# A 128-token output product of the last stage cut into four column tiles of 32 tokens

## The chip, the core and the metric

The kernel runs on one core of a Trainium2 chip. The core has a matrix engine (PE, with a separate record PEld for the loading of its stationary operand), three elementwise engines (DVE, ACT, POOL), and a DMA queue issued by SyncE (SP). The metric is the device time of one execution in microseconds (us); lower is better.

## The reference

The input is 8192 tokens of 512 channels, all float32. What is computed, cut to its core:

```
h = layernorm(x) * (1 + ca) + sa
y = state_space_scan(h)                 # one 16 x 16 recurrence for each channel
y = gelu(layernorm(y)*ln_w + ln_b)
x = x + ga * (h + y @ W_out.T + b_out)  # the first output product is y @ W_out.T
h = layernorm(x) * (1 + cb) + sb
x = x + gb * ffn(h)                     # 512 -> 64 channels, 16 relus for each, -> 512
```

ca, sa, ga, cb, sb, gb come from a small product of silu(c) with a 512 x 3072 matrix.

## The kernel before

The first stages (until about 488 us) turn the scan into matrix products: powers of the 16 x 16 matrices, taps, states at chunk borders, and a banded product for each channel. They leave y for all tokens in SBUF.

The last stage runs over 32 units u of 256 tokens, two tiles t of 128 tokens each. It is a software pipeline written out by hand: each engine has its own list in program order, and semaphores tie them. ACT normalises y (L512), PE transposes it (`t_y`, L1019, line 1019), ACT applies gelu into `zT` (L520, channels on partitions, tokens in columns). PE then forms the first output product, `out1` (L1029): for each tile of 128 tokens, four matmuls over the four groups q of 128 channels, stationary operand `zT` (128 channels x 128 tokens), moving operand `WoT` (128 channels x 512 outputs), accumulated in one PSUM bank, 2 + t, with the tokens on the partitions. DVE adds the residual (L798). The second half normalises again (L529), transposes (`t_x`, L1052), multiplies by a 512 x 64 matrix (`s_prod`, L1062), evaluates 16 relus (ACT L547, DVE L828), and multiplies by the 64 x 512 matrix (`out2`, L1071). Biases are added by bfloat16 matmuls of 32 rows (`bias_pair`, L1037 and L1041; L1075).

PE's list for unit u is: out1 of tile 0 (q = 0 to 3); transposes `t_x` of unit u - 2; out2 and its bias of unit u - 6; out1 of tile 1, q = 0, 1; transposes `t_y` of unit u + 1, first half; the bias pair; out1 of tile 1, q = 2, 3; `t_y`, second half; and after every odd unit from 3 on, `s_prod` of two units. Parts whose unit does not exist are left out at both ends.

A matmul addresses a part of PE's 128 x 128 array. The trace writes that part as rows*columns: 128*128 is the whole array, 128*32 a column tile 32 wide, whose output lies on 32 PSUM partitions; 128*64 is half the columns; 64*128 and 32*128 are row tiles, for products over 64 or 32 channels. Every float32 matmul shows as two records in the trace, called passes here, each with its own weight load; a bfloat16 one shows as one.

Of the kernel before, what the change touches and what calls it, by code (L numbers as in the profile page):

```python
# [12 lines left out]
P = 128  # L13
# [18 lines left out]
QB = D // P  # L32
# [12 lines left out]
BR = 32  # L45
# [13 lines left out]
def adaln_ssm_kernel(nc, x_in, A_in, Bm_in, Cm_in, Dm_in, lnw_in, lnb_in, Wo_in, bo_in,  # L59
# [12 lines left out]
    with ctx:  # L72
# [15 lines left out]
        def pair_of(i):  # L88
            return XY[:, :, i, :, :].rearrange("p b c a -> p b (c a)")

        def channel(d):
            return XY[:, :, d // 2, :, d % 2]
# [51 lines left out]
        zT = A0[:, 0:2048].rearrange("p (r q t) -> p r q t", r=2, q=QB)  # L144
# [9 lines left out]
        WoT = C0[:, 2048:4096].rearrange("p (q d) -> p q d", q=QB)  # L154
# [27 lines left out]
        PS = ctx.enter_context(nc.psum_tensor("PS", [P, 8, 512], f32))  # L182

        def pv_ps(r):
            return PS[:, 2 * r:2 * r + 2, :].rearrange("p b (s w) -> p (b s) w", w=128)

        def w_ps(r):
            return PS[:, 4 + r, :].rearrange("p (g w) -> p g w", w=64)
# [673 lines left out]
        def _(pe):  # L862
# [16 lines left out]
            for half in range(HALVES):  # L879
# [4 lines left out]
                for n in range(STEPS):  # L884
# [10 lines left out]
                    for j in range(8):  # L895
                        g = 8 * o + j
                        for e in QD:
                            pe.matmul(pv_ps(r)[e:e + BW, j, 0:w + NS], BDTs[e:e + BW, b, j, :], PV[e:e + BW, g, PW - w:PW + NS],  # L898
                                      start=True, stop=True)
                        for e in QD:  # L900
                            mm = pe.matmul(w_ps(r)[e:e + BW, j, 0:w], BDs[e:e + BW, b, j, :], WP[e:e + BW, g, L + 1 - w:L + 1],  # L901
                                           start=True, stop=True)
# [4 lines left out]
                for b in range(2):  # L907
                    for m in range(4):
                        for e in range(4):
                            g = (4 * b + e) * 4 + m  # L910
                            mm = pe.matmul(PS[32 * e:32 * e + 32, 4, b * P:(b + 1) * P], CM[:, g, :], PV[:, g, 0:L],
                                           start=(m == 0), stop=(m == 3))
# [3 lines left out]
                for g in range(HG):  # L916
                    for e in QD:
                        mm = pe.matmul(PS[e:e + BW, 5, g:g + 1], BDs[e:e + BW, (base + STEPS + g // 8) % BDR, g % 8, :],
                                       WP[e:e + BW, g, L:L + 1], start=True, stop=True)
# [14 lines left out]
                for q in range(8):  # L934
# [6 lines left out]
                    for i in range(4):  # L941
                        for e in range(4):
                            d = (half * HG + 4 * q + i) * GC + 2 * e
                            mm = pe.matmul(PS[32 * e:32 * e + 32, q % 4, i * P:(i + 1) * P],
                                           Uring[:, q % 2, i * P + 32 * e:i * P + 32 * e + 32], pair_of(d // 2),
                                           start=True, stop=True)
                    mm.then_inc(S["u_mm"], 1)
                    if q == 4:
                        pe.wait_ge(S["ksa_r"], 2 * (half + 1))
                        for b in range(2):  # L950
                            mm = pe.transpose(PS[:, 4, HD + b * P:HD + (b + 1) * P], ktsa[:, b, :], ident[:, :])
# [6 lines left out]
                for i in range(SSTEPS):  # L958
# [6 lines left out]
                    for j in range(8):  # L965
                        g = 8 * o + j
                        for e in QD:
                            mm = pe.matmul(pv_ps(n % 2)[e:e + BW, j, 0:NS + NC], BDTs[e:e + BW, n % BDR, j, :],  # L968
                                           PV[e:e + BW, g, H0:PW + NS], start=True, stop=True)
# [4 lines left out]
                for g in range(HG):  # L974
                    n = half * HG + g
                    if half == HALVES - 1 and 6 <= g < 6 + QB:
                        q = g - 6
# [3 lines left out]
                        for o in range(QB):  # L981
                            mm = pe.transpose(PS[:, 6 + q % 2, o * P:(o + 1) * P], WoN[:, o, q * P:(q + 1) * P], ident[:, :])
                        mm.then_inc(S["wo_tr"], 1)
                    if half == HALVES - 1 and g == 18:

                        pe.wait_ge(S["ld_w"], 16 * 15)
                        for r in range(2):
                            for q in range(QB):
                                mm = pe.matmul(PS[64 * r:64 * r + 64, 5, 0:1], WinS[:, q, :], cbsb[:, 4 + q:5 + q], start=(q == 0), stop=(q == QB - 1))
# [9 lines left out]
                    for h in range(GC):  # L999
                        for a in range(0, P, 64):  # L1000
                            mm = pe.matmul(PS[a:a + 64, g % 4, h * NC:(h + 1) * NC], Tring[:, n % 3, h, a:a + 64], channel(n * GC + h),  # L1001
                                           start=False, stop=(h == GC - 1), skip_group_check=True)
# [19 lines left out]
            def out1(u, t, qs):  # L1022
                n = TPU * u + t
                if t == 1 and qs[0] == 0 and u >= 1:
                    pe.wait_ge(S["x2_r"], n - TPU + 1)
                for q in qs:
                    if t == 0 and q % 2 == 0:
                        pe.wait_ge(S["gelu_r"], QB * u + q + 2)
                    mm = pe.matmul(PS[:, 2 + t, :], zT[:, u % 2, q, t * P:(t + 1) * P], WoT[:, q, :], start=(q == 0 and t == 1),  # L1029
                                   stop=(q == QB - 1))  # L1030
                if qs[-1] == QB - 1:
                    mm.then_inc(S["o1_mm"], 1)

# [46 lines left out]
            for u in range(NU + LAG):  # L1080
                w = u - 1
                if u < NU:
                    out1(u, 0, (0, 1, 2, 3))
                if 1 <= w <= NU:
                    t_x(w - 1, 0)
                    t_x(w - 1, 1)
                if u >= LAG:
                    out2(u - LAG)
                if u < NU:
                    out1(u, 1, (0, 1))  # L1090
                if u + 1 < NU:
                    t_y(u + 1, 0)
                if u < NU:
                    bias_pair(u)
                    out1(u, 1, (2, 3))
                if u + 1 < NU:
                    t_y(u + 1, 1)
                if w % 2 == 0 and 2 <= w <= NU:
                    s_prod(w - 2)
                    s_prod(w - 1)  # L1100
# [33 lines left out]
```

## Time and profile before

| | |
|---|---|
| three runs | 897.92, 901.37, 901.39 us; median 901.37 |
| the profiled execution's own time | 900.21 us |
| its span, first to last instruction | 898.5 us (1.7 us lie around it) |
| PE busy / weight loads busy | 823.3 us (92%) / 553.7 us (62%) |
| DVE, ACT, POOL busy | 570.9, 415.2, 487.9 us |
| mean granted clock of TensorE | 0.909 |
| L1029, passes | 512 |

The span is from the first to the last instruction. A start in the trace is a time measured; the end of a matmul is modelled and reaches into the next one, so that the durations of adjoining PE rows overlap. To know what a group of matmuls occupies, subtract its start from the start of the next row.

### The profile page before, as it was taken

How to read it: one execution, taken by the hardware profiler on the slowest of the kernel's cores; microseconds unless marked ns; L12 is line 12 of the kernel's file. 1: busy time of each engine (PE TensorE's matmuls, PEld its weight loads, DVE VectorE, ACT ScalarE, POOL GpSimd, SP SyncE). 2: the span in 40 equal slices, each digit the busy share in tenths (PEclk: the TensorE clock that was granted, in tenths of full speed). 3: DMA queues.
4: the chain of work that ended last, by engine and by line, in shares of the span. 5: the costliest groups of instructions: out<-in, count | busy, mean ns of one | idle time of the engine just before them, and what ended most of it. 6: DMA issues, size and time to landing. Idle time of an engine off the chain costs nothing.

```text
span 898.5 us, 24744 instructions
## 1 busy us (share of the span) xinstructions
PE 823.3 (92%) x10139; PEld 553.7 (62%) x10139; DVE 570.9 (64%) x1264; ACT 415.2 (46%) x887; POOL 487.9 (54%) x643
## 2 busy tenths in 40 slices
PE   1999978999979999888995999999999999999983
PEld 1967876866669999686663455555555455555540
DVE  5768658833331224883479347877787777777765
ACT  2645632100001113210000569788777788777763
POOL 3634441744433233174443989777777777777500
PEclk9999779999975558999998899999999999999975
DMA  8954302059820000206985220222222222221112
GB/s 249 392 165 148 94 6 85 3 150 249 243 56 3 2 2 4 61 3 191 272 232 184 82 94 2 94 94 94 92 81 87 94 87 79 95 93 48 47 71 94
DMA packets 109808, 94.88 MB, mean 106 GB/s; under 512 B 14976, under 2 KB 81152, under 8 KB 109696
## 3 DMA queue, kind: packets, MB, share of 16 engines
q1 hardware_dynamic: 109696, 93.31, 32.8%
q8 instruction: 80, 1.31, 0.6%
q14 instruction: 32, 0.26, 0.1%
HBM read 75.99 MB, written 17.30 MB: 104 GB/s over the span
## 4 chain that ended last, share of the span: by engine, by line
PE 77%; DVE 11%; DMA 3%; issue 3%; POOL 2%; ACT 2%; SPq 1%; DVEq 0%; POOLq 0%; ACTq 0%
PE PS L1029 26%; PE PS L898 9%; PE PS L901 7%; PE PS L1001 5%; PE PS L996 4%; PE PS L968 4%; PE PS L1062 4%; PE PS L1071 4%; PE PS L1019 3%; PE PS L876 3%; PE PS L1052 3%; DMA arenaC<-kernel_taps 2%; DVE arenaA L750 2%; DVE arenaA L756 1%; DVE arenaC L640 1%
## 5 line engine op out<-in xcount | busy, mean ns | idle before, releaser
L1029 PE MATMUL PS<-arenaC,arenaA 128*128 128x512 f32 x512 | 244.0, 610 | 0.0
L358 POOL TENSOR_TENSOR arenaC<-arenaA,par 128x512 f32<-128x512 f32 x104 | 107.7, 1040 | 145.9 <-ACT arenaA L482 70.5
L898 PE MATMUL PS<-arenaA,arenaC 64*64 64x17 f32 (+6 forms) x1792 | 160.3, 261 | 23.8 <-DVE arenaC L640 23.8
L898 PEld LDWEIGHTS PS<-arenaA,arenaC 64*64 64x64 f32 x1792 | 136.4, 192 | 29.2 <-issue 24.4
L901 PE MATMUL PS<-arenaA,arenaC 64*64 64x1 f32 (+6 forms) x1792 | 152.2, 239 | 0.0
L1029 PEld LDWEIGHTS PS<-arenaC,arenaA 128*128 128x128 f32 x512 | 90.1, 190 | 94.2 <-issue 89.7
L901 PEld LDWEIGHTS PS<-arenaA,arenaC 64*64 64x64 f32 x1792 | 137.4, 192 | 0.0
L828 DVE SCALAR_TENSOR_TENSOR PS<-arenaA,ffc,PS 128x256 f32<-128x256 f32 x224 | 109.2, 487 | 41.5 <-ACT arenaA L547 22.7
L640 DVE STREAM_TRANSPOSE arenaC<-arenaC 128x512 f32<-128x512 f32 x104 | 73.5, 707 | 93.1 <-POOL arenaC L358 92.0
L547 ACT ACTIVATE arenaA<-PS,ffc 128x256 f32<-128x256 f32 x256 | 124.9, 582 | 8.8 <-PE PS L1062 7.8
L408 POOL TENSOR_TENSOR arenaC<-arenaA,mask 128x504 f32<-128x504 f32 x64 | 65.9, 1031 | 77.2 <-PE PS L996 74.8
L652 DVE TENSOR_TENSOR XY<-PS,arenaA 128x256 f32<-128x256 f32 x128 | 48.4, 420 | 77.3 <-PE PS L1001 76.9
L1001 PEld LDWEIGHTS PS<-XY,arenaC 128*64 128x64 f32 x2048 | 65.9, 136 | 51.0 <-issue 34.9
L520 ACT ACTIVATE arenaA<-PS,lnwb 128x256 f32<-128x256 f32 x128 | 65.9, 575 | 52.4 <-PE PS L1019 52.3
L512 ACT ACTIVATE arenaC<-XY,sy 128x512 f32<-128x512 f32 x64 | 49.2, 821 | 83.0 <-POOL sy L344 83.0
L424 POOL TENSOR_TENSOR ROWS<-ROWS 128x512 f32<-128x512 f32 x64 | 81.5, 1273 | 5.3
L1001 PE MATMUL PS<-XY,arenaC 128*64 128x64 f32 x2048 | 74.8, 224 | 2.2 <-DMA arenaC<-kernel_taps 2.2
L996 PE MATMUL PS<-arenaC,arenaA 128*128 128x512 f32 x128 | 71.6, 641 | 1.6 <-DVE arenaA L1109 1.6
L480 ACT ACTIVATE arenaA<-PS 128x128 f32<-128x128 f32 x56 | 15.5, 278 | 122.3 <-PE PS L901 122.3
L968 PE MATMUL PS<-arenaA,arenaC 64*64 64x80 f32 x1536 | 60.4, 231 | 11.3 <-DVE arenaA L1109 5.9
L968 PEld LDWEIGHTS PS<-arenaA,arenaC 64*64 64x64 f32 x1536 | 56.5, 133 | 15.7 <-issue 11.0
L1019 PEld LDWEIGHTS PS<-ident,arenaC 128*128 128x128 f32 x256 | 32.5, 143 | 43.3 <-issue 43.3
(154 smaller groups left out, 1206.0 us busy)
## 6 DMA issues: line engine op xcount, KB each, us to landing
arenaC<-kernel_taps SPq DMA_DIRECT2D x64, 512.0 KB, 4.3
arenaC<-in_L_attn_x SPq DMA_DIRECT2D x32, 256.0 KB, 4.4
XY<-in_L_attn_x SPq DMA_DIRECT2D x32, 256.0 KB, 4.4
arenaC<-in_L_attn_x SPq DMA_DIRECT2D x15, 512.0 KB, 3.5
out<-arenaC SPq DMA_DIRECT2D x15, 512.0 KB, 2.7
XY<-in_L_wmod SPq DMA_DIRECT2D x6, 1024.0 KB, 8.1
XY<-in_L_attn_x SPq DMA_DIRECT2D x11, 512.0 KB, 3.6
out<-XY SPq DMA_DIRECT2D x11, 512.0 KB, 2.8
```

What stands on the lines that cost most here:

```text
L358: gp.tensor_tensor(BDs[:, step % BDR, :, :].rearrange("p g (a m) -> p g a m", m=NS), src, msk, ALU.mult).then_inc(S["bdp_r"], 1)
L408: gp.tensor_tensor(BDH[:, g % 2, :, 1:NC], PV[:, g, H0:H0 + NC - 1].unsqueeze(1).to_broadcast([P, GC, NC - 1]), mask8[:, :].unsqueeze(2).t ...
L424: chain(gp.tensor_tensor(tmp, tmp, Grow, ALU.mult))
L547: act.activation(rr[:, h % RELU_RING, :], PS[:, 5, 0:FP * P], ACT.Relu, scale=W1c[:, h:h + 1], bias=b1c[:, h:h + 1]).then_inc(S["relu_r"], 1)
L640: dve.transpose(BDTs[:, step % BDR, :, :], BDs[:, step % BDR, :, :]).then_inc(S["bdt_r"], 1)
L828: ins = dve.scalar_tensor_tensor(out=dst, in0=rr[:, h % RELU_RING, :], scalar=W2c[:, h:h + 1], in1=g, op0=ALU.mult, op1=ALU.add)
L898: pe.matmul(pv_ps(r)[e:e + BW, j, 0:w + NS], BDTs[e:e + BW, b, j, :], PV[e:e + BW, g, PW - w:PW + NS], start=True, stop=True)
L901: mm = pe.matmul(w_ps(r)[e:e + BW, j, 0:w], BDs[e:e + BW, b, j, :], WP[e:e + BW, g, L + 1 - w:L + 1], start=True, stop=True)
L968: mm = pe.matmul(pv_ps(n % 2)[e:e + BW, j, 0:NS + NC], BDTs[e:e + BW, n % BDR, j, :], PV[e:e + BW, g, H0:PW + NS], start=True, stop=True)
L996: pe.matmul(PS[:, g % 4, :], WP[:, g, 0:L], BDH[:, g % 2, :, :], start=True, stop=False, skip_group_check=True).then_inc(S["o_mm"], 1)
L1001: mm = pe.matmul(PS[a:a + 64, g % 4, h * NC:(h + 1) * NC], Tring[:, n % 3, h, a:a + 64], channel(n * GC + h), start=False, stop=(h == GC - ...
L1029: mm = pe.matmul(PS[:, 2 + t, :], zT[:, u % 2, q, t * P:(t + 1) * P], WoT[:, q, :], start=(q == 0 and t == 1), stop=(q == QB - 1))
```

## The change

Each matmul of `out1`, with its 128 tokens, becomes four matmuls in a loop over a = 0, 32, 64, 96. Each takes 32 columns of `zT` as its stationary operand and the same 512 outputs of `WoT` as its moving operand, and writes PSUM partitions a to a + 31 of the same bank. The four go to four column tiles of the array. Bias, semaphores, the flags for the start and stop of an accumulation, and the other engines' lists are as they were. The loop covers both tiles t of every unit: 256 matmuls become 1024.

```
                 for q in qs:
                     if t == 0 and q % 2 == 0:
                         pe.wait_ge(S["gelu_r"], QB * u + q + 2)
-                    mm = pe.matmul(PS[:, 2 + t, :], zT[:, u % 2, q, t * P:(t + 1) * P], WoT[:, q, :], start=(q == 0 and t == 1),
-                                   stop=(q == QB - 1))
+                    for a in range(0, P, BR):
+                        mm = pe.matmul(PS[a:a + BR, 2 + t, :], zT[:, u % 2, q, t * P + a:t * P + a + BR], WoT[:, q, :],
+                                       start=(q == 0 and t == 1), stop=(q == QB - 1))
                 if qs[-1] == QB - 1:
                     mm.then_inc(S["o1_mm"], 1)
```

PE's list before, in an even unit of the steady state, from the first matmul of `out1` of tile 0 to the transposes after the second half of tile 1 (the numbers after the tile names are the output's partitions x its columns; brackets name semaphores waited for):

```order
L1029 MATMUL PS<-arenaC,arenaA 128x512 [waits gelu_r]
L1029 MATMUL PS<-arenaC,arenaA 128x512
L1029 MATMUL PS<-arenaC,arenaA 128x512 [waits gelu_r]
L1029 MATMUL PS<-arenaC,arenaA 128x512
L1052 MATMUL PS<-ident,arenaA 128x128 [waits gelu_r,xh2_r]
...
L1075 MATMUL PS<-bcs,ones_bf 128x512 x2
L1029 MATMUL PS<-arenaC,arenaA 128x512 [waits x2_r]
L1029 MATMUL PS<-arenaC,arenaA 128x512
L1019 MATMUL PS<-ident,arenaC 128x128 [waits xT_r,yh_r]
```

The same places of PE's list in the changed kernel, where the lines from `out1` on have a number one higher:

```order
L1030 MATMUL PS<-arenaC,arenaA 32x512 [waits gelu_r]
L1030 MATMUL PS<-arenaC,arenaA 32x512 x7
L1030 MATMUL PS<-arenaC,arenaA 32x512 [waits gelu_r]
L1030 MATMUL PS<-arenaC,arenaA 32x512 x7
L1053 MATMUL PS<-ident,arenaA 128x128 [waits gelu_r,xh2_r]
...
L1076 MATMUL PS<-bcs,ones_bf 128x512 x2
L1030 MATMUL PS<-arenaC,arenaA 32x512 [waits x2_r]
L1030 MATMUL PS<-arenaC,arenaA 32x512 x7
L1019 MATMUL PS<-ident,arenaC 128x128 [waits xT_r,yh_r]
```

Nothing changes its place and no wait is added. Each block of `out1` has four times the instructions, of another shape than the transposes on either side of it.

## Rows read from the trace of the kernel before

**Rows 1.** The page: busy share, and the clock, in 40 slices of the span.
```profile
PE   1999978999979999888995999999999999999983
...
PEclk9999779999975558999998899999999999999975
```

**Rows 2.** Busy time of every engine in stretches of the last stage; start:end length, engines, clock.
```profile
core 0: us, PE busy (x) PEld busy (x) DVE busy (x) ACT busy (x) POOL busy (x), PEclk, DMA share, GB/s
...
500.00:600.00 100.00, 100.00 (x437) 51.86 (x436) 68.00 (x147) 74.70 (x138) 86.34 (x116) 1.00 0.17 56
...
800.00:858.00 58.00, 58.00 (x262) 29.13 (x260) 42.20 (x88) 45.24 (x87) 36.75 (x50) 1.00 0.16 57
```

**Rows 3.** Waits from 480 to 870 us: waiter <- waited for: us, times, longest.
```profile
ACT arenaA L520 <- PE PS L1019: 52.3, 46, 5.1
...
DVE arenaC L798 <- PE PS L1029: 25.9, 14, 8.4
```

**Rows 4.** PE in order of time, two units of the steady state: start, us, what, count.
```profile
600.17 0.60 PE L1019 MATMUL PS<-ident,arenaC 128*128 128x128 f32 x4
600.70 1.97 PE L1062 MATMUL PS<-arenaA,WinS 128*64 128x128 f32 x32
602.60 3.70 PE L1029 MATMUL PS<-arenaC,arenaA 128*128 128x512 f32 x8
606.13 1.04 PE L1052 MATMUL PS<-ident,arenaA 128*128 128x128 f32 x8
607.10 1.13 PE L1071 MATMUL PS<-ROWS 64*128 64x512 f32 x4
...
611.15 1.98 PE L1029 MATMUL PS<-arenaC,arenaA 128*128 128x512 f32 x4
612.97 0.60 PE L1019 MATMUL PS<-ident,arenaC 128*128 128x128 f32 x4
613.41 3.60 PE L1029 MATMUL PS<-arenaC,arenaA 128*128 128x512 f32 x8
616.84 1.04 PE L1052 MATMUL PS<-ident,arenaA 128*128 128x128 f32 x8
```

**Rows 5.** PE in order of time, the products in four column tiles (L944).
```profile
142.45 1.08 PE L944 MATMUL PS<-XY,arenaC 128*32 128x128 f32 x32
143.46 0.44 PE L951 MATMUL PS<-ident,arenaC 128*128 128x128 f32 x2
...
370.55 0.66 PE L927 MATMUL PS<-ident,arenaA 128*128 128x128 f32 x4
371.13 1.95 PE L944 MATMUL PS<-XY,arenaC 128*32 128x128 f32 x64
373.02 0.70 PE L955 MATMUL PS<-arenaC,WinS 128*128 128x256 f32 x2
```

**Rows 6.** Weight loads of the same stretch.
```profile
371.13 1.69 PEld L944 LDWEIGHTS PS<-XY,arenaC 128*32 128x32 f32 x64 [0.17 <-issue]
```

**Rows 7.** PE in order of time, the products in two column tiles (L1001).
```profile
476.44 1.16 PE L1001 MATMUL PS<-XY,arenaC 128*64 128x64 f32 x32
477.54 1.12 PE L996 MATMUL PS<-arenaC,arenaA 128*128 128x512 f32 x2
```

**Rows 8.** PE in order of time, the early units, without out2.
```profile
518.29 1.04 PE L1052 MATMUL PS<-ident,arenaA 128*128 128x128 f32 x8
519.16 1.88 PE L1029 MATMUL PS<-arenaC,arenaA 128*128 128x512 f32 x4
520.88 0.60 PE L1019 MATMUL PS<-ident,arenaC 128*128 128x128 f32 x4
```

**Rows 9.** PE in order of time, the end of the last unit.
```profile
856.55 1.98 PE L1029 MATMUL PS<-arenaC,arenaA 128*128 128x512 f32 x4
858.47 1.97 PE L1062 MATMUL PS<-arenaA,WinS 128*64 128x128 f32 x32
860.37 1.09 PE L1052 MATMUL PS<-ident,arenaA 128*128 128x128 f32 x8
861.39 1.13 PE L1071 MATMUL PS<-ROWS 64*128 64x512 f32 x4
```

**Rows 10.** The chain that ended last: start, us, what.
```profile
858.54 1.92 PE PS L1062 x32
860.48 1.21 ACT arenaA L547 x3
```

## The prediction

> **What bounds the kernel now.** I read the slices of the page first. From the stage's start at about 494 us to about 860 us PE stands at nine tenths or more in every slice, and the clock is at its upper level, 2.4 GHz, except in the slice where the stage starts and in those of the drain [rows 1]. Next the busy times by stretch: from 500 to 858 us PE is busy for every microsecond at a granted clock of 1.00, DVE at 68 to 73%, ACT at 75 to 78%, POOL at 63 to 86% [rows 2]. A PE that is busy by modelled ends is not yet a PE that bounds, so I asked who waits for whom: ACT's gelu waits for PE's transposes for 52.3 us, and DVE's residual for this very product for 25.9 us [rows 3]. Then PE in order of time, by starts. A block of eight passes of L1029 takes 616.84 - 613.41 = 3.43 us, 0.43 us a pass; four passes of a transpose take 613.41 - 612.97 = 0.44 us, 0.11 us a pass [rows 4]. 512 and 128 columns at two cycles of 2.4 GHz each are 0.427 and 0.107 us, so PE streams without a bubble. The other engines follow it, and what PE's list gains or loses here goes to the span unchanged. At the end nothing takes it back: the chain leaves PE at the last L1062, and the relus of ACT start from its end [rows 10].
>
> **What an even spread over column tiles costs.** The work streamed is unchanged: 256 matmuls of 128 tokens become 1024 of 32, and 512 passes become 2048, in 512 groups of four that should run side by side. The nearest rows are L944, the same form with 128 columns in place of 512, four tiles of 128*32. 32 passes take 143.46 - 142.45 = 1.01 us and 64 take 373.02 - 371.13 = 1.89 us [rows 5]. The 32 passes more are eight groups, 0.88 / 8 = 0.11 us a group, just what one pass over the whole array takes for 128 columns [rows 4]. Four column tiles share neither the array nor the stream. So a group of four with 512 columns should take the 0.43 us of one pass now, and the stream costs nothing. Extrapolating the length by four is my choice; the trace has no column tile with 512 columns. Its lower bound is the same 0.43, for no tiled row streams a column in less than two cycles (the pairs of L1001, 64 columns, take about 0.056 us: 1.10 us less 0.2 for the change of shape, over 16 pairs [rows 7]). Its upper bound I take from the start to start distance that four tiles would add if it weren't overlapped, 0.02 us a group, 10 us in all; L944 shows none of it in 16 groups.
>
> **What the changes of shape cost.** Here the rows speak plainly.
> Leaving a shape: four transposes before another L1029 take 0.44 us, four before L1062, which uses the array as 128*64, take 600.70 - 600.17 = 0.53 [rows 4]. A change costs 0.09 us, though both shapes have all 128 rows.
> Entering one: the first weight load of the new shape isn't hidden. L1029 after L1062 takes 606.13 - 602.60 = 3.53 us for eight passes, against 3.43 after transposes: 0.10 us [rows 4]. Transposes after L1062 take 861.39 - 860.37 = 1.02 us [rows 9], after L1029 607.10 - 606.13 = 0.97 [rows 4], both before the same L1071: 0.05 us.
> A block in four column tiles: twice 1.01 less 1.89 leaves 0.13 us a block, for its entry and its exit together [rows 5]. Of it 0.09 is the change at its end; 0.04 is the short load of 32 columns and the four starts apart.
>
> The Trainium skill says the same in TensorEngine Tiling (Array Packing), Key Properties, and it speaks against this change: going from one tile to another of the same mode is free, a change of the mode drains TensorE. It gives no price. By that rule alone, at the 0.09 us of the row, the new changes of shape listed below (21 at an entry, 92 at an exit, of which the tiled block's 0.13 holds its own) would cost 10.2 us, near my sum.
>
> **The sum.** PE's list has 94 blocks of `out1`: 2 of 12 passes (units 0 and 1), 30 of 8 (tile 0), 62 of 4 (tile 1). Four groups:
> 71 blocks come today after another shape (57 after the biases, 14 after L1062) and before transposes of their own shape. They pay 0.10 at the entry today and 0.13 afterwards: 71 x 0.03 = 2.1 us.
> 21 come after transposes of the same shape: the 12 of unit 1, 16 of the blocks of 8, and 4 of the early units, where no out2 stands between (1.72 us for four passes, nothing beside the stream [rows 8]). The transposes ahead of them now pay 0.09 for leaving and the block 0.13, where nothing was paid: 21 x 0.22 = 4.6 us.
> 2 in the last unit stand between two changes already: 858.47 - 856.55 = 1.92 us for four passes, 0.20 over the stream [rows 9]; 0.13 in its place gives back 0.1 us.
> 92 are followed by transposes, which pay 0.05 for their own first load: 4.6 us.
> Together 2.1 + 4.6 - 0.1 + 4.6 = 11.2 us. Starts are rounded to 0.01 us, so the sum could be about 1 us off either way. The first block runs at the lower clock, which doubles one entry and is nothing. All of it lies on PE's list between 497 and 860 us, beside nothing. Nobody else is queued anew: ACT's and DVE's lists are the same, and both have slack. The sum is against the profiled execution's 900.21 us: 911.4. The runs' median, 901.37, lies 1.2 us above that execution, so the median of the changed kernel should come out near 912.5, which I forecast.
> Bounds: below, if the transposes' load is hidden after all (4.6 less) and the exit costs what it does from 128*64, 907 from the same base; above, with 0.02 us a group lost to the stagger, 922.
>
> **The rivals.**
> Weight loads stand in line. The four tiles use the same 128 rows, and if a load can't pass running matmuls that use these rows, each of the 418 groups inside a block would wait for it: L944's 0.04 us a block, less the starts apart, is about 0.03 us a load, 12 us more, 924. For it: nothing in a row. Against it: L944's 64 loads lie within 1.69 us, under 64 passes that take no longer than their stream [rows 5, 6]; a pair of L1001 with two loads of 64 columns takes 0.056 us, so loads run side by side as well [rows 7]. Chance 5%.
> The Trainium skill has the rule behind this rival, in TensorE: Matmul & The Clock Gate, Part 3: a weight load overlaps running matmuls only where the row group differs. Here no row group differs; by the rule the time would be 924, and L944 disagrees with it.
>
> The streams don't fit four abreast. L944 reads 128 columns at a time; with 512 the four streams might serialise into two pairs. Every group would take 0.86 us: 512 x 0.43 = 220 us more, 1130. L944's stream is without a gap over 16 groups, and I see no reason for a longer one to differ. Chance 2%.
>
> It gets faster. The one saving in the rows is the entry: the load of a 32-column tile exposes 0.03 to 0.04 us where the whole width exposes 0.10, at 73 blocks, about 5 us. If going into and out of a column tile drained nothing, and the transposes' load hid under the last streams, only that saving would be left: 901.4 - 5 = 896. It decides if an exit and the load behind it cost under about 0.02 us together. Against it: 128*128 to 128*64 is such a change of columns alone, and costs 0.09 [rows 4]; L944 holds 0.13 a block [rows 5]. Chance 2%.
>
> PE's extra time falls into waits: then 901. PE waits for nobody here by its starts, so only the tail could hide it, and that starts from PE [rows 10]. Chance 2%.
>
> A partial cover, some loads hidden beside the drain, gives 905 to 908. Chance 8%. My forecast, with 908 to 917 around it, has the remaining 81%.
>
> **Range and chances.** 8 in 10 with both near neighbours: 907.5 to 920. A measurement of this kernel tells 0.5% from nothing, 4.5 us. Slower: forecast, partial cover but for its lower edge, weight loads in line and serial streams, 95%. Same: 3%, hidden time and that edge. Faster: 2%.
>
> **What would show it.** In the profile after: 2048 passes of 128*32 for the product; eight groups of four in a block of tile 0 from start to start in about 3.43 + 0.13 = 3.56 us, before and after s_prod alike, where it is 3.53 or 3.43 now; the transposes ahead of it 0.53 in every unit; the transposes after it 0.05 longer than now; two units together about 0.7 us longer; PE still 100% busy between 500 and 865 us at a clock of 1.00; the time from the end of the last block of the product to the end of the span as long as now, 898.5 - 858.5 = 40 us. If a block of tile 0 takes 3.8 us, it is the loads; if 7, the streams. I am wrong if a block of eight groups takes under 3.4 us, or if PE shows waits for ACT or DVE in the steady state.

## The result and the profile after

Four runs of the changed kernel took 909.03 to 914.06 us, median 912.06; four of the kernel before, on the same chip, 897.92 to 901.39, median 900.45. The ratio is 1.0131, 95% interval 1.0093 to 1.0168: slower by 1.3%, 11.6 us between the medians. The profiled execution took 912.76 us, its span 911.0 (before 900.21 and 898.5). The forecast was a median of 912.5.

The busy times by stretch, of the changed kernel (columns as in [rows 2]):

```profile
500.00:600.00 100.00, 100.00 (x874) 38.56 (x868) 63.17 (x137) 70.93 (x131) 83.30 (x114) 1.00 0.16 57
...
800.00:858.00 58.00, 58.00 (x510) 23.89 (x513) 41.81 (x90) 45.73 (x87) 42.24 (x58) 1.00 0.16 56
```

They answer to [rows 2]: PE is still never idle, at a granted clock of 1.00. In the first stretch ACT and DVE have a smaller share than before, since they do the same work behind a slower PE. PEld falls from 51.86 to 38.56 us there, and that is no gain: loads under running passes cost nothing before either.

The waits in the changed kernel from 480 to 880 us (total, times, longest), and then the product's group before and after (busy us, mean ns | idle before):

```profile
ACT arenaA L520 <- PE PS L1019: 61.4, 48, 4.8
DVE arenaC L798 <- PE PS L1030: 28.0, 14, 8.1
```

```profile
L1029 PE MATMUL PS<-arenaC,arenaA 128*128 128x512 f32 x512 | 244.0, 610 | 0.0
L1030 PE MATMUL PS<-arenaC,arenaA 128*32 128x512 f32 x2048 | 240.2, 599 | 0.0
```

ACT waits 9 us longer for PE than in [rows 3]. The product's own busy time went *down*, 244.0 to 240.2 us, while the kernel got slower: a busy time of modelled ends says nothing here. What does is the starts, PE in order of time, in the changed kernel:

```profile
605.83 0.66 PE L1019 MATMUL PS<-ident,arenaC 128*128 128x128 f32 x4
606.42 1.97 PE L1063 MATMUL PS<-arenaA,WinS 128*64 128x128 f32 x32
608.31 3.64 PE L1030 MATMUL PS<-arenaC,arenaA 128*32 128x512 f32 x32
611.88 1.09 PE L1053 MATMUL PS<-ident,arenaA 128*128 128x128 f32 x8
612.91 1.13 PE L1072 MATMUL PS<-ROWS 64*128 64x512 f32 x4
...
614.29 1.92 PE L1030 MATMUL PS<-arenaC,arenaA 128*32 128x512 f32 x16
616.14 0.66 PE L1019 MATMUL PS<-ident,arenaC 128*128 128x128 f32 x4
...
618.91 0.66 PE L1019 MATMUL PS<-ident,arenaC 128*128 128x128 f32 x4
619.50 3.64 PE L1030 MATMUL PS<-arenaC,arenaA 128*32 128x512 f32 x32
623.07 0.66 PE L1053 MATMUL PS<-ident,arenaA 128*128 128x128 f32 x4
```

Subtract each start from the next, and compare with [rows 4]. Eight groups of four take 611.88 - 608.31 = 3.57 us behind s_prod (3.53 before) and 623.07 - 619.50 = 3.57 behind transposes (3.43 before). Four groups take 1.85. So 4 more groups take 3.57 - 1.85 = 1.72 us, 0.43 each: the four tiles run abreast for 512 columns too, and each block pays 0.14 once. Eight transposes behind the product take 1.03 (0.97 before). Four of them take 0.59 ahead of another shape; between two blocks of the product they took 0.44.

The weight loads show the entry directly. First the kernel before, then the changed one, in both the first loads of `t_x` (L1052, L1053) behind the product:

```profile
605.71 0.14 PEld L1052 LDWEIGHTS PS<-ident,arenaA 128*128 128x128 f32 x1 [0.24 <-issue]
606.13 0.80 PEld L1052 LDWEIGHTS PS<-ident,arenaA 128*128 128x128 f32 x7 [0.29 <-issue]
```

```profile
611.88 0.86 PEld L1053 LDWEIGHTS PS<-ident,arenaA 128*128 128x128 f32 x8 [0.84 <-issue]
```

Before, the first of the eight loads starts at 605.71, under the product's last pass and 0.42 us ahead of the first transpose at 606.13. Behind the column tiles no load starts early: all eight stand at or behind the first transpose at 611.88.

For the comparisons below I use one stretch of steady state, 28 units: from the second half of unit 4's transposes to the end of the last block of the product. Its ends, first in the kernel before, then in the changed one:

```profile
532.69 0.49 PE L1019 MATMUL PS<-ident,arenaC 128*128 128x128 f32 x3
...
858.47 0.33 PE L1062 MATMUL PS<-arenaA,WinS 128*64 128x128 f32 x2
```

```profile
535.83 0.44 PE L1019 MATMUL PS<-ident,arenaC 128*128 128x128 f32 x2
...
872.03 0.44 PE L1063 MATMUL PS<-arenaA,WinS 128*64 128x128 f32 x4
```

325.78 us before, 336.20 after: 10.42 us in 14 pairs of units, 0.74 a pair. Of the span's 12.5 us, 1.5 more lie in the first units of the stage, 1.6 in the stages ahead, which the change doesn't touch, and the tail is 1.0 shorter (39.0 for 40.0). Those last two are of the size by which executions of the same code differ there. In the six profiled executions of before, after, e1, e2a, e2b and e3 the code ahead of the stage is the same, and the stage's first transpose starts between 494.55 and 499.14 us; in all of these but e3 the tail's code is the same too, and it took 38.3 to 40.0 us. So the steady stretch is the better ruler: where PE has no gap, nearly all blocks of the same kind in the same surroundings agree to 0.01 us.

### The profile page after: what moved, and what is told of

Its sections match the earlier page's. It is cut to its first block, busy times and chain, and to the rows that moved or that the text cites. A ratio compares the mean times of both kernels' runs of the same rounds, so it can differ in the third digit from the quotient of the medians.

```text
span 911.0 us, 27816 instructions
## 1 busy us (share of the span) xinstructions
PE 837.8 (92%) x11675; PEld 517.4 (57%) x11675; DVE 571.0 (63%) x1264; ACT 416.7 (46%) x887; POOL 489.0 (54%) x643
## 4 chain that ended last, share of the span: by engine, by line
PE 80%; DVE 10%; issue 3%; DMA 2%; POOL 2%; ACT 2%; SPq 1%; DVEq 0%; POOLq 0%; ACTq 0%
PE PS L1030 26%; PE PS L898 10%; PE PS L901 7%; PE PS L1001 5%; PE PS L996 5%; PE PS L968 4%; PE PS L1019 4%; PE PS L1072 3%; PE PS L1063 3%; PE PS L1053 3%; PE PS L876 3%; DVE arenaA L750 2%; DMA arenaC<-kernel_taps 1%; DVE arenaA L756 1%; DVE arenaC L640 1%
## 5 line engine op out<-in xcount | busy, mean ns | idle before, releaser
L1030 PE MATMUL PS<-arenaC,arenaA 128*32 128x512 f32 x2048 | 240.2, 599 | 0.0
L898 PE MATMUL PS<-arenaA,arenaC 64*64 64x17 f32 (+6 forms) x1792 | 163.7, 265 | 21.1 <-DVE arenaC L640 21.1
L901 PE MATMUL PS<-arenaA,arenaC 64*64 64x1 f32 (+6 forms) x1792 | 155.2, 242 | 0.0
L898 PEld LDWEIGHTS PS<-arenaA,arenaC 64*64 64x64 f32 x1792 | 138.8, 195 | 26.6 <-issue 23.1
L901 PEld LDWEIGHTS PS<-arenaA,arenaC 64*64 64x64 f32 x1792 | 140.0, 196 | 0.0
L1030 PEld LDWEIGHTS PS<-arenaC,arenaA 128*32 128x32 f32 x2048 | 57.0, 109 | 117.3 <-issue 111.5
L1001 PEld LDWEIGHTS PS<-XY,arenaC 128*64 128x64 f32 x2048 | 66.0, 136 | 50.7 <-issue 35.7
L1001 PE MATMUL PS<-XY,arenaC 128*64 128x64 f32 x2048 | 74.9, 224 | 2.0 <-DMA arenaC<-kernel_taps 1.8
L996 PE MATMUL PS<-arenaC,arenaA 128*128 128x512 f32 x128 | 71.6, 641 | 1.6 <-DVE arenaA L1110 1.6
L480 ACT ACTIVATE arenaA<-PS 128x128 f32<-128x128 f32 x56 | 15.5, 277 | 124.7 <-PE PS L901 124.7
L968 PEld LDWEIGHTS PS<-arenaA,arenaC 64*64 64x64 f32 x1536 | 57.7, 135 | 15.8 <-issue 10.8
L1019 PEld LDWEIGHTS PS<-ident,arenaC 128*128 128x128 f32 x256 | 27.6, 143 | 62.5 <-issue 62.5
```

Of the source, the lines that this page charges most:

```text
L996: pe.matmul(PS[:, g % 4, :], WP[:, g, 0:L], BDH[:, g % 2, :, :], start=True, stop=False, skip_group_check=True).then_inc(S["o_mm"], 1)
L1030: mm = pe.matmul(PS[a:a + BR, 2 + t, :], zT[:, u % 2, q, t * P + a:t * P + a + BR], WoT[:, q, :], start=(q == 0 and t == 1), stop=(q == QB ...
```

## The experiments

Theory: each change of the array's shape costs, at the exit about 0.095 us, at the entry an exposed weight load that grows with the tile's width. Rival: column tiles cost something for each group or instruction. The steady stretch is read from one profiled execution of each kernel; the last column compares its runs with runs of the kernel before on the same chip.

The expectations up to v3 name a stretch of 361.5 us, the whole product, from its first matmul to the end of its last. It holds the stage's first block, part of which runs at the lower clock and which alone took 5.97 us in v1, 6.53 before and 7.36 in e2a, so I use the steady stretch beside it.

| kernel | steady stretch, us | against before | runs, ratio to before |
|---|---|---|---|
| before | 325.78 | | |
| after | 336.20 | +10.42 | 1.0131 [1.0093, 1.0168] |
| e2a, tiles in 14 even units | 327.07 | +1.30 | 1.0016 [0.9991, 1.0041] |
| e2b, tiles in 14 odd units | 329.70 | +3.92 | 1.0039 [1.0018, 1.0061] |
| e1, two tiles of 64 | 334.98 | +9.20 | 1.0128 [1.0097, 1.0159] |
| e3, s_prod in four tiles too | 334.03 | +8.25 | 1.0104 [1.0065, 1.0143] |
| v1, bias of 64 rows | 323.11 | -2.67 | 0.9955 [0.9930, 0.9979] |
| v2, bias pair behind out2 | 330.69 | +4.92 | 1.0077 [1.0048, 1.0105] |
| v3, bias closes tile 0, ahead of out2 | 318.32 | -7.46 | 0.9918 [0.9885, 0.9950] |
| v4, bias closes tile 0, behind out2 | 315.20 | -10.58 | 0.9866 [0.9833, 0.9900] |
| e4, four column tiles in v4 | 330.60 | +4.82 | 1.0077 [1.0046, 1.0108] |

**Same work, two places: e2a and e2b.** Both cut 14 blocks of tile 0 into column tiles and differ only in what stands ahead.

Against the changed kernel, e2a (the statement's last line is left out):

```
-                    for a in range(0, P, BR):
-                        mm = pe.matmul(PS[a:a + BR, 2 + t, :], zT[:, u % 2, q, t * P + a:t * P + a + BR], WoT[:, q, :],
+                    cw = BR if t == 0 and u % 2 == 0 and u >= 4 else P
+                    for a in range(0, P, cw):
+                        mm = pe.matmul(PS[a:a + cw, 2 + t, :], zT[:, u % 2, q, t * P + a:t * P + a + cw], WoT[:, q, :],
```

e2b differs in one line:

```
+                    cw = BR if t == 0 and u % 2 == 1 and u >= 5 else P
```

> Column tiles only in the block of tile 0 of the 14 even units from 4 on, which stands behind s_prod and so behind another shape already. My theory, changes of shape: 14 x (0.035 at the block + 0.055 at the transposes behind it) = +1.3 us over before on the stretch from the first matmul of the product to the end of its last (361.5 us before). Rival, a cost for each group of four tiles (12.0 us over 512 groups = 0.023 us a group): 14 x 8 x 0.023 = +2.6 us, the same as for the odd units.

> The same number of column-tiled matmuls, 14 blocks of tile 0, but in the odd units from 5 on, whose block stands behind transposes of the whole array. Changes of shape: 14 x (0.095 at the transposes ahead + 0.135 at the block + 0.055 behind) = +4.0 us on the same stretch, three times what the even units cost. Rival, a cost for each group: +2.6 us as for the even units.

On the steady stretch, which holds all 28 blocks in question, +1.30 and +3.92 us: the theory's two numbers, three to one, where the rival has one number for both. PE in order of time, e2a with a tiled and an untiled block, then e2b with a tiled one:

```profile
606.39 1.97 PE L1064 MATMUL PS<-arenaA,WinS 128*64 128x128 f32 x32
608.28 3.64 PE L1031 MATMUL PS<-arenaC,arenaA 128*32 128x512 f32 x32
611.86 1.10 PE L1054 MATMUL PS<-ident,arenaA 128*128 128x128 f32 x8
...
618.75 0.60 PE L1019 MATMUL PS<-ident,arenaC 128*128 128x128 f32 x4
619.19 3.60 PE L1031 MATMUL PS<-arenaC,arenaA 128*128 128x512 f32 x8
622.62 1.04 PE L1054 MATMUL PS<-ident,arenaA 128*128 128x128 f32 x8
```

```profile
614.54 0.60 PE L1019 MATMUL PS<-ident,arenaC 128*128 128x128 f32 x4
615.07 3.64 PE L1031 MATMUL PS<-arenaC,arenaA 128*32 128x512 f32 x32
618.64 1.09 PE L1054 MATMUL PS<-ident,arenaA 128*128 128x128 f32 x8
```

The tiled block is 3.57 to 3.58 us in either place; it is the neighbours that differ. In e2b the transposes ahead take 0.53 where e2a's untiled unit has 0.44, and the block they lead to had cost 3.43, not 3.53. Over the whole product, the stretch that the two expectations name, e2a is 2.1 us longer than before and e2b 3.5. The first block of the product makes the difference: it took 6.53 us before, 7.36 in e2a and 6.11 in e2b, and neither edit touches it. It stands where the clock rises: the granted clock was 0.54 from 495 to 500 us before, and still 0.50 from 500 to 505 us in e2a. With it taken out the two come to 1.3 and 3.9 us again.

**Two tiles of 64: e1.** M is 64. Against the changed kernel:

```
-                    for a in range(0, P, BR):
-                        mm = pe.matmul(PS[a:a + BR, 2 + t, :], zT[:, u % 2, q, t * P + a:t * P + a + BR], WoT[:, q, :],
+                    for a in range(0, P, M):
+                        mm = pe.matmul(PS[a:a + M, 2 + t, :], zT[:, u % 2, q, t * P + a:t * P + a + M], WoT[:, q, :],
```

> The product in two column tiles of 64 tokens in place of four of 32. Changes of shape: they stay, only the exposed load at a block's entry doubles in width (0.03 to 0.05) and two starts in place of four lie apart, so a block costs 0.155 to 0.16 over its stream in place of 0.14: the stretch is 1.5 us longer than with four tiles, about 375 us, time about 1.015 of before. Rival, a cost for each tile or instruction: half the tiles, half the 12 us, 367.5 us.

The rival falls: half the tiles leave the cost where it was, 9.2 of 10.4 us. My own number was off as well. The whole product's stretch came out at 372.2, 1.2 us shorter than with four tiles, where I had it 1.5 longer. In order of time:

```profile
607.46 1.97 PE L1063 MATMUL PS<-arenaA,WinS 128*64 128x128 f32 x32
609.25 3.60 PE L1030 MATMUL PS<-arenaC,arenaA 128*64 128x512 f32 x16
612.79 1.09 PE L1053 MATMUL PS<-ident,arenaA 128*128 128x128 f32 x8
...
620.42 3.65 PE L1030 MATMUL PS<-arenaC,arenaA 128*64 128x512 f32 x16
624.00 0.77 PE L1053 MATMUL PS<-ident,arenaA 128*128 128x128 f32 x5
```

Behind transposes the block takes 3.58 us, as forecast a little over four tiles. Behind s_prod it takes 3.54, and s_prod itself 1.79 in place of 1.89: s_prod is 128*64 too, so in e1 the two share a shape, and I had left that out. 14 times 0.15 us, 2.1 us, is most of the 2.8 us that I was off by. The theory holds, I had misapplied it.

**Give the neighbour the same shape: e3.** This is the same effect made on purpose.

```
                     for t in range(TPU):
-                        mm = pe.matmul(PS[M * t:M * t + M, 5, (u % FP) * P:(u % FP + 1) * P], WinS[:, q, :],
-                                       x2T[:, u % 2, q, t * P:(t + 1) * P], start=(q == 0), stop=(q == QB - 1))
+                        for a in range(0, M, BR):
+                            mm = pe.matmul(PS[M * t + a:M * t + a + BR, 5, (u % FP) * P:(u % FP + 1) * P], WinS[:, q, a:a + BR],
+                                           x2T[:, u % 2, q, t * P:(t + 1) * P], start=(q == 0), stop=(q == QB - 1))
```

> The changed kernel, and s_prod too in four column tiles of 128*32 (two token tiles x two halves of its 64 outputs), so that the product of the 14 even units stands behind its own shape. Changes of shape: s_prod loses its exit (0.095) and half its exposed load (0.03), the product behind it its entry (0.03): 14 x 0.155 = 2.2 us off the changed kernel's stretch of 373.5, so 371.3; a block of 32 passes of s_prod becomes 64 and takes 1.77 us in place of 1.90, the product's block behind it 3.54 in place of 3.57. Rival, a cost for each tile: s_prod's 240 pairs become as many groups of four, +0.02 each, so 5 us more, 378.

```profile
605.37 1.95 PE L1064 MATMUL PS<-arenaA,WinS 128*32 128x128 f32 x64
607.14 3.62 PE L1030 MATMUL PS<-arenaC,arenaA 128*32 128x512 f32 x32
610.68 1.09 PE L1053 MATMUL PS<-ident,arenaA 128*128 128x128 f32 x8
```

1.77 us for s_prod and 3.54 for the block behind it, both as forecast, and 2.17 us less than the changed kernel on the steady stretch (forecast 2.2). The whole product took 371.9 us for a forecast of 371.3, with 6.87 us in its first block where the changed kernel had 6.27. Twice the instructions in s_prod made PE faster.

**Remove changes that the kernel before has: v1 to v4.** If changes of shape are what costs, the kernel before has some to give back. All four start from it. v1 (cut at the dots):

```
-    chain(dve.tensor_tensor(em[:, 4:7], ident[:, 0:3], ident[:, BR:BR + 3], ALU.add))
+    chain(dve.tensor_tensor(em[:, 4:7], ident[:, 0:3], ident[:, M:M + 3], ALU.add))
...
-    pe.matmul(PS[:, 3, :], ones_bf[0:BR, :], bias1[0:BR, :], start=False, stop=False)
+    pe.matmul(PS[:, 3, :], ones_bf[0:M, :], bias1[0:M, :], start=False, stop=False)
```

and likewise for the other three bias matmuls, whose rows start at M instead of BR.

> From the kernel before (whole-array product). The bias matmuls take 64 rows in place of 32 (rows beyond the three parts of the bias are zero), so that the bias behind out2 has out2's shape, 64*128. If a change of shape is what costs, and float32 to bfloat16 alone doesn't: out2's four passes lose 0.095 us of their 1.06, in 26 units: -2.5 us on the stretch of 361.5, about 0.3% of the time. If the change of type costs as much: nothing.

Before, then v1:

```profile
607.10 1.13 PE L1071 MATMUL PS<-ROWS 64*128 64x512 f32 x4
608.16 0.39 PE L1075 MATMUL PS<-bcs,ones_bf 32*128 32x512 bf16 x2
608.48 1.98 PE L1029 MATMUL PS<-arenaC,arenaA 128*128 128x512 f32 x4
```

```profile
603.77 1.13 PE L1071 MATMUL PS<-ROWS 64*128 64x512 f32 x4
604.73 0.38 PE L1075 MATMUL PS<-bcs,ones_bf 64*128 64x512 bf16 x2
605.04 1.98 PE L1029 MATMUL PS<-arenaC,arenaA 128*128 128x512 f32 x4
```

out2's four passes take 0.96 us in place of 1.06, and 2.67 us are gone (forecast 2.5). The change from float32 to bfloat16 in one shape costs nothing here; the one from 64 rows to 32 did.

In v2 the bias pair moves behind out2 as well. The pair's first matmul, no longer out1, then starts the accumulation in bank 3 and waits for the residual of tile 1 of the unit before; those lines are left out here.

```
                 if u < NU:
+                    bias_pair(u)
                     out1(u, 1, (0, 1))
                 if u + 1 < NU:
                     t_y(u + 1, 0)
                 if u < NU:
-                    bias_pair(u)
                     out1(u, 1, (2, 3))
```

> v1, and the bias pair of each unit stands right behind out2 and its bias, in the same shape. Each steady unit loses one stay in another shape: the exit of the transposes (0.097), the exit of the pair (0.100) and the exposed load of the product behind it (0.107), 0.30 us x 26 = 7.9 us, with v1's 2.5 about 10 us, stretch 351, time about 890. Against it: the pair waits for DVE's residual of tile 0, which in odd units ends 0.8 us behind that place now: 13 x 0.8 = 10 us back, stretch 361, no change.

```profile
601.26 0.38 PE L1039 MATMUL PS<-b1f,ones_bf 64*128 64x512 bf16 x1
602.32 0.39 PE L1043 MATMUL PS<-b1f,ones_bf 64*128 64x512 bf16 x1 [0.68 <-DVE XY L798]
...
614.50 0.38 PE L1077 MATMUL PS<-bcs,ones_bf 64*128 64x512 bf16 x2
614.72 0.38 PE L1039 MATMUL PS<-b1f,ones_bf 64*128 64x512 bf16 x1
```

The changes are saved (the pair stands 0.22 us behind its neighbour of the same shape), and the kernel is slower, 4.9 us on the steady stretch and 7.1 on the whole product's, 368.6 us, where I had 351 to 361. The pair's second matmul waits for DVE's residual of tile 0, more than the 0.8 us a time that I had allowed. Its idle time, 0.68 us where it shows, understates it: start to start the matmul stands 1.06 us behind the one ahead, in most odd units. The pairs of the steady stretch occupy 24.3 us, and 8.8 in v4, where they stand in the same place without the wait: 15.5 us lost for 10.6 saved.

v3 and v4 take that wait away: the bias of tile 0 is no longer laid down a unit ahead, but closes tile 0's accumulation. The new pair (its wait and out1's changed flags are left out):

```
+                pe.matmul(PS[:, 2, :], ones_bf[M:2 * M, :], bias1[M:2 * M, :], start=False, stop=True).then_inc(S["o1_mm"], 1)
+                pe.matmul(PS[:, 3, :], ones_bf[0:M, :], bias1[0:M, :], start=True, stop=False)
```

PE's order in v3 is out1 of tile 0, bias pair, out2, t_x, out1 of tile 1. In v4 it is out1 of tile 0, t_x, out2, bias pair, out1 of tile 1, and DVE takes the residual of out2 ahead of that of tile 0.

> As v2, but the pair of a unit stands right behind its own tile 0, then out2 and its bias, then t_x; the bias of tile 0 closes its accumulation, so nothing waits for DVE's residual of the same unit. Changes of shape: 10 us less than before as in v2, and the load at the entry of the product behind t_x is hidden too (t_x pays 0.05 in its place), stretch 350, time about 889. Against it: t_x stands 1.5 us later, and if ACT then comes late with its columns for s_prod, PE waits, up to 1 us a unit.

> As v3, but t_x keeps its place behind tile 0, then out2, its bias and the unit's bias pair, all in 64*128; DVE takes tile 0's residual behind that of out2. One stay in another shape a unit. Changes of shape: 10.4 us off before on the steady stretch (from the start of the eighth block of transposes to the end of the last block of the product, 325.8 us before): 315.4, without v3's wait of 0.42 us every second unit, time about 0.988 of before. Rival: DVE's residual of tile 0, 2 us later, makes PE wait at the next tile 0; then 318 or more and idle time at L1029.

v3 saves 7.5 us but misses its forecast: the whole product takes 354.9 us for 350, and the steady stretch stops at 318.3, 3.1 us short of v4. Its transposes ahead of the next tile 0 take 0.85 us in place of 0.44 in every second unit, and PE waits for ACT's gelu, 0.42 us each time, 5.8 us on the stretch; I had named the risk, but at s_prod. ACT's list has its wait for t_x ahead of that gelu, 57.7 us in all between 520 and 850 us, where ACT's own gelu waits for PE 3.6 us. That this wait is what makes gelu late is read from ACT's order and wasn't tried apart; v4, which puts t_x back, doesn't show the gap.

```profile
616.19 0.60 PE L1019 MATMUL PS<-ident,arenaC 128*128 128x128 f32 x4
617.04 3.67 PE L1029 MATMUL PS<-arenaC,arenaA 128*128 128x512 f32 x8 [0.25 <-ACT arenaA L520]
```

v4 reaches 315.20 (forecast 315.4) without a gap, and is 1.3% faster than the kernel before: 888.67 us median in six runs against 899.39, ratio 0.9866 [0.9833, 0.9900].

```profile
608.61 3.60 PE L1029 MATMUL PS<-arenaC,arenaA 128*128 128x512 f32 x8
612.04 1.04 PE L1050 MATMUL PS<-ident,arenaA 128*128 128x128 f32 x8
613.01 1.13 PE L1069 MATMUL PS<-ROWS 64*128 64x512 f32 x4
613.97 0.38 PE L1073 MATMUL PS<-bcs,ones_bf 64*128 64x512 bf16 x2
614.19 0.38 PE L1039 MATMUL PS<-b1f,ones_bf 64*128 64x512 bf16 x1
...
614.50 1.98 PE L1029 MATMUL PS<-arenaC,arenaA 128*128 128x512 f32 x4
```

**The same edit in v4: e4.** The loop over four column tiles, now in v4.

> The change under study (four column tiles) made in v4, where fewer blocks of the product stand behind another shape. Changes of shape: the last block of tile 1 now also stands between transposes, so two units cost 0.285 + 0.09 + 2 x (0.09 + 0.285) = 1.13 us over v4, in 15.5 pairs 17.4 us, where the same edit cost 10.4 us in the kernel before (336.2 against 325.8 us). Rival, a cost of the column tiles themselves: the same 10.4 us as before, whatever stands around them.

+15.40 us over v4 on the steady stretch, where the same edit cost 10.42. A price of the tiles themselves would be the same in both. The theory's 1.13 us a pair makes 15.8 us in the 14 pairs that the stretch holds; I had multiplied by 15.5, more than the stretch holds.

## Why the prediction was right

Time 912.06 for 912.5, inside the range, with the mechanism forecast. That the two agree to 0.4 us is partly luck. The forecast stands on the median of three runs, 901.37, and with the fourth that is 900.45, so 11.1 us were forecast and 11.6 came. The runs of either kernel lie 3.5 to 5 us apart, and 1.6 and -1.0 us of the profiled difference lie where the change does nothing. The steps are better judged by the starts:

*PE bounds, and nothing hides its extra time.* Right: no idle time of PE between the first and the last block of the product in either profile. The shares of the other engines were read too low: [rows 2] shows two of the four stretches, and from 600 to 800 us DVE is busy for 79 to 80% and ACT for 81%, above the 68 to 73% and 75 to 78% that the prediction gives. PE waits for neither there, so nothing hangs on it.

*The stream costs nothing.* Right, and this was the step that rested on a choice, four times the longest column-tiled stream in the trace. A group takes 0.43 us; no stagger builds up: 0.14 us over the stream for blocks of 4 and of 8 groups alike. Nothing is left for the upper bound of 0.02 us a group.

*Prices.* Leaving 0.09: right (0.59 - 0.06 - 0.44 for the transposes). Transposes' load 0.05: 0.06 measured (1.03 against 0.97). A tiled block 0.13: 0.14 measured. For the whole product the sum was 11.2 us and 12.0 came (361.5 to 373.5 us: 496.96 to 858.47 before, 498.56 to 872.03 after), 0.8 us more, within the 1 us allowed for rounding. The prices were rounded down. With those of the experiments' forecasts (0.035 for a block that stood behind another shape, 0.095 + 0.135 for one behind its own, 0.055 for the transposes behind) the same counts give 2.5 + 4.8 - 0.1 + 5.1 = 12.3 us; the first block, where the clock rises, took 6.27 us for 6.53 and gives 0.3 back.

*The rivals.* Weight loads in line: no, blocks take 3.57, not 3.8. Streams in pairs: no, a group takes 0.43, not 0.86. Faster through short loads: the saving is real (0.03 at the entry for 0.10), and it is eaten where the prediction said, by the exit and by the load behind it. Hidden time: none. Partial cover: none either, the exit and the transposes' load both show in full in e2b.

*What the profile would show.* One sign was wrong in its wording: I said that the transposes ahead of tile 0 would take 0.53 in every unit. They stand behind a tiled block too, and pay their own load: 0.59. The sum had counted that load. The stretch from the product's end to the end of the span came out at 39.0 us, not as long as the 40 of before; that is inside what unchanged code shows.

## What to carry to other kernels

Cutting this full-size product into tiles that run abreast gained nothing in the stream, and since its neighbours on the matrix engine have another shape it paid twice at each block, for leaving the shape and for the first weight load of the next. So count the changes of shape in a dense list, not the instructions, and price them by the starts: here 0.1 to 0.2 us each, about a hundred of them, decided the time in both directions (v4 is the other one). Put work of one shape together, widen a small matmul with zero rows to its neighbour's shape, and check who the moved work then waits for: v2 saved the same changes as v4 and lost more to one wait.

## What the runs showed of the hardware

The exposed load at an entry goes by the tile's width: 0.03 us for 32 columns (s_prod in e3: 1.77 us over a stream of 16 x 0.109 = 1.74), 0.05 for 64 (e1's s_prod, 1.79), 0.10 for the whole width (the product behind s_prod, 3.53 for 3.43). Two kinds of work don't fit that. The transposes' load is 128 columns wide and costs 0.05 to 0.06 us (1.03 for 0.97). The bfloat16 pair of biases pays next to nothing at its entry: 0.32 us behind another shape with its exit of 0.095 (608.16 to 608.48 before), so some 0.22, and 0.22 behind its own shape (613.97 to 614.19 in v4). Why wasn't tried.

An exit costs 0.09 to 0.10 us whether rows or columns change: the transposes take 0.53 for 0.44 ahead of 128*32 (e2b), and out2's four passes 1.06 ahead of 32*128 for 0.96 ahead of 64*128 (before and v1). A change of type in one shape costs nothing that shows.

A wider row tile is free: the bias over 64 rows takes 0.31 us in v1 (604.73 to 605.04), over 32 rows 0.32 before, the exit in both.

In executions of unchanged code the tail differs by up to 1.7 us and the start of the stage by up to 4.6. What the record shows of it is that longer runs have a lower mean granted clock: of the 19 runs of the kernel before beside e1, e2 and e3, the shortest, 895.86 us, has 0.913 and the longest, 903.87 us, 0.907. Which stage loses the clock, and why, wasn't tried.
